# A two-layer transformer kernel: the first layer's attention outputs kept by feature, their division by the softmax sums moved to the next stage

## What is computed

```
def _attn(x, ctx, wq, wk, wv, wo, bo, heads):
    ...
    q = (x @ wq).reshape(b, n, heads, dh).transpose(0, 2, 1, 3)
    k = (ctx @ wk).reshape(b, j, heads, dh).transpose(0, 2, 1, 3)
    v = (ctx @ wv).reshape(b, j, heads, dh).transpose(0, 2, 1, 3)
    a = jax.nn.softmax(jnp.einsum('bhid,bhjd->bhij', q, k) * scale, axis=-1)
    out = jnp.einsum('bhij,bhjd->bhid', a, v)
    out = out.transpose(0, 2, 1, 3).reshape(b, n, heads * dh)
    return out @ wo + bo
...
x = _attn(h1, h1, q1, k1, v1, o1_w, o1_b, heads) + x
...
x = _attn(h2, context, q2, k2, v2, o2_w, o2_b, heads) + x
...
ff = a * jax.nn.gelu(g, approximate=False) @ ff_w2 + ff_b2
```

## Time and profile before

| | us |
|---|---|
| median of 3 runs (lowest, highest) | 3342.19 (3334.15, 3347.52) |
| the profiled execution, its time | 3342.7 |
| its span in the trace | 3341.0 |
| self-attention, from about 207 to 698 | 491 |
| q stage, 698 to 852 | 154 |
| cross-attention, 852 to 1029 | 177 |
| ff stage, 1029 to 1700 | 671 |
| layer 1, 1700 to 3341 | 1641 |

### The profile page before, as it was taken

How to read it: one execution, slowest core, us unless ns; L and a number is a source line. 1 busy time by engine, 2 the same in 40 slices (tenths; PEclk the granted TensorE clock), 3 DMA queues, 4 the chain that set the end, 5 groups by cost and what they waited for, 6 DMA issues and landing times. The chain is left out here.

```text
span 3341.0 us, 47964 instructions
## 1 busy us (share of the span) xinstructions
PE 2936.9 (88%) x15594; PEld 1775.7 (53%) x15594; DVE 2157.7 (65%) x3834; ACT 1892.4 (57%) x3214; POOL 805.5 (24%) x1149
## 2 busy tenths in 40 slices
PE   6989999978696999998959999879978577899999
PEld 5754444457455888886731111111126342788888
DVE  5668888837453444444649999968868685444443
ACT  4328888844353232233549999989975355333322
POOL 2021221114640000000027888200003471200000
PEclk9969999989798999998975555555559898899999
DMA  8663333336762000001567557266723213010000
GB/s 228 211 166 101 106 107 103 90 80 158 165 176 46 10 10 19 9 0 38 152 173 163 128 137 164 32 90 83 97 56 96 79 45 92 26 36 18 25 17 16
DMA packets 358243, 296.57 MB, mean 89 GB/s; under 512 B 175602, under 2 KB 281914, under 8 KB 358058
## 3 DMA queue, kind: packets, MB, share of 16 engines
q1 hardware_dynamic: 347994, 273.93, 34.0%
q0 software_dynamic: 7280, 18.07, 2.1%
q10 hardware_dynamic: 2784, 2.29, 0.4%
HBM read 177.53 MB, written 114.52 MB: 87 GB/s over the span
## 5 line engine op out<-in xcount | busy, mean ns | idle before, releaser
L1591 PE MATMUL nat<-k_stack,q_stack 48*128 48x512 bf16 x640 | 381.0, 605 | 71.5 <-DMA k_stack<-k1w 31.1
L1391 DVE TENSOR_REDUCE neg_max<-nat 128x1 f32<-128x512 f32 x640 | 400.7, 682 | 61.3 <-PE nat L1250 61.2
L1625 DVE TENSOR_REDUCE m_all<-nat 128x1 f32<-128x512 f32 x640 | 423.3, 691 | 18.1 <-PE nat L1591 17.8
L804 POOL TENSOR_TENSOR rstd<-var_eps,neghalf 128x4 f32<-128x4 f32 x48 | 51.9, 1081 | 1588.0 <-DVE var_eps L1028 1588.0
L1645 ACT ACTIVATE nat<-nat,m_all 128x512 f32<-128x512 f32 x640 | 427.7, 2130 | 3.0 <-DVE m_all L1625 2.9
L1645 ACT ACTIVATION_READ_ACCUMULATOR nat<-nat,m_all 128x1 f32 x640 | 403.6, 1674 | 0.0
L1054 DVE SCALAR_TENSOR_TENSOR ff<-outp,bias,gel 128x512 f32<-128x512 f32 x160 | 120.1, 751 | 417.6 <-PE outp L326 417.6
L1325 ACT ACTIVATE probs<-sT 128x1024 f32<-128x1024 f32 x320 | 328.0, 1027 | 93.1 <-PE sT L1259 85.5
L968 ACT ACTIVATE gel<-outp,bias 128x512 f32<-128x512 f32 x160 | 110.0, 688 | 351.6 <-PE outp L326 351.6
L1839 ACT ACTIVATE exps<-sT 128x1024 f32<-128x1024 f32 x320 | 293.4, 1573 | 10.5 <-PE sT L1788 10.5
L972 ACT CAST ff_hi<-ff 128x512 fp32r<-128x512 f32 x160 | 99.2, 620 | 312.3 <-DVE ff L1054 312.3
(11 more groups left out here) (561 smaller groups left out, 7163.3 us busy)
## 6 DMA issues: line engine op xcount, KB each, us to landing
v<-vpad SPq DMA_DIRECT2D x64, 320.0 KB, 2.8
q_stack<-q_part SPq DMA_DIRECT2D x90, 160.0 KB, 5.8
k_stack<-k1w SPq DMA_DIRECT2D x90, 160.0 KB, 10.5
q_stack<-q_hi SPq DMA_DIRECT2D x160, 64.0 KB, 2.5
v_stack<-v SPq DMA_DIRECT2D x40, 256.0 KB, 3.2
q_stack<-q_hi SPq DMA_DIRECT2D x80, 128.0 KB, 2.8
raw<-v SPq DMA_DIRECT2D x16, 640.0 KB, 14.9
k_stack<-k_hi SPq DMA_DIRECT2D x158, 64.0 KB, 2.2
```

What stands on the lines that cost most here:

```text
L1391: dve.tensor_reduce(neg_max[:, n % 2, qt, 2 * pr + ab:2 * pr + ab + 1], nat[(16 * (n + 2) + t) % 3][:, :], AX.X, ALU.max, negate=True).the ...
L1591: pe.matmul(bank[i % NAT][:, :], q_stack[half, slot, g, pr, qt * P:(qt + 1) * P], k_stack[half, slot, g, pr, :], start=True, stop=True).th ...
L1625: dve.tensor_reduce(k.m_all[:, column(i // TILES, i % TILES)], bank[i % NAT][:, :], AX.X, ALU.max, negate=True).then_inc(s["e_max_ready"], 1)
```

## The change

Both attentions of layer 0 stop after `o_ps`: it is copied to a now double `o_sb` (by ACT in self-attention, by DVE in cross-attention) and stored as it is, 128 rows of 2 KB per quad, the sums and padding among them. The transposes, the second copy, the per-quad reciprocal and the multiply go. Instead, once per sample, a DMA loads the 20 rows of sums as an 80x128 tile (`load_sums`), DVE inverts it (`invert`), and another DMA stores it (`store_shares`); these two DMAs are SP's in self-attention and POOL's in cross-attention. In cross-attention the loads of v move from SP's list to POOL's.

The q stage and the ff stage take the form by feature. For each sample SP issues eight DMAs: four bring the output (`attn_T`), four bring the inverted sums, each head's row sent to 16 partitions (`shares`). DVE multiplies the two in three steps of 128x512 (`scale`) before the high and low halves are taken. The twelve transposes of each sample go.

```diff
+        scale = [("scale", m) for m in range(3)] if recips is not None else []
...
-            ahead = {"oT": 1, "oproj": 1, "stats": 1, "norm": 1, "zT": 1, "tail": -1}
-            between = [[("tail", 0)], oT[0:2], oT[2:], oproj[0:2], oproj[2:], [("stats", 0)], [("norm", 0)],
+            ahead = {"oT": 1, "oproj": 1, "stats": 1, "norm": 1, "zT": 1, "tail": -1, "scale": 1}
+            between = [[("tail", 0), *scale], oT[0:2], oT[2:], oproj[0:2], oproj[2:], [("stats", 0)], [("norm", 0)],
...
+            if scale:
+                ahead["scale"] = 3
             body = [("stats", 0), *oT[0:2], items[0], oT[2], ("norm", 0), items[1], items[2], oproj[0], ("double", 0),
-                    zT[0], zT[1], oproj[1], zT[2], oproj[2], oproj[3]]
+                    zT[0], zT[1], oproj[1], zT[2], *scale[0:2], oproj[2], *scale[2:], oproj[3]]
...
-            n_attn = 3 if by_feature else TT + 1
+            n_attn = 8 if scale else 3 if by_feature else TT + 1
+            if scale:
+                shares = sb("shares", [P, 3, TOK])
...
+                    if scale:
+                        heads = rows(attn_in, b * (QUADS * P), QUADS * P).rearrange("(h c) t -> h c t", c=VCOL)[:, 0:DH, :]
+                        spread = rows(recips, b * HEADS, HEADS).unsqueeze(1).broadcast_to([HEADS, DH, TOK])
+                        for tile, src in ((attn, heads), (shares, spread)):
+                            for c in range(2):
+                                sp.dma_start(tile[:, c, :], src[8 * c:8 * c + 8]).then_inc(s["attn_in_loaded"], 16)
+                            for half in range(2):
+                                sp.dma_start(tile[64 * half:64 * half + 64, 2, :], src[16:HEADS]
+                                             ).then_inc(s["attn_in_loaded"], 16)
+                        return
...
+                        elif scale:
+                            act.wait_ge(s["o_scaled"], at["o_scaled"] + b * 3 + m + 1)
...
-                    if kind == "oT":
+                    if kind == "scale":
+                        if m == 0:
+                            dve.wait_ge(s["attn_in_loaded"],
+                                        at["attn_in_loaded"] + b * (16 * n_attn) + 16 * n_attn)
+                        dve.tensor_tensor(attn[:, m, :], attn[:, m, :], shares[:, m, :], ALU.mult
+                                          ).then_inc(s["o_scaled"], 1)
+                    elif kind == "oT":
...
-        recip = sb("recip", [P, 2, TT, 4])
-        o_sb, o_turned = sb("o_sb", [P, TOK]), sb("o_turned", [P, 2, TOK])
-        o_nat = sb("o_nat", [P, 2, TT, 4, DH])
+        o_sb = sb("o_sb", [P, 2, TOK])
+        sums, shares = sb("sums", [TT * HEADS, P]), sb("shares", [TT * HEADS, P])
...
+                def load_sums(b):
+                    for r in range(2):
+                        wait(sp, f"a_o_stored{r}", 16 * ((QUADS * (b + 1) - r + 1) // 2))
+                    sums_of = rows(out, b * (QUADS * P), QUADS * P).rearrange("(h c) t -> h c t", c=VCOL)[:, DH, :]
+                    sp.dma_start(sums[:, :], sums_of.rearrange("h (x t) -> h x t", t=P)
+                                 ).then_inc(s["a_sums_loaded"], 16)
+
+                def store_shares(b):
+                    wait(sp, "a_recip", b + 1)
+                    sp.dma_start(rows(recips, b * HEADS, HEADS).rearrange("h (x t) -> h x t", t=P), shares[:, :]
+                                 ).then_inc(s["a_recip_stored"], 16)
...
-                    if exists(n - 3):
-                        wait(sp, "a_o_normed", n - 2)
-                        sp.dma_start(rows(out, (n - 3) * TOK, TOK).rearrange("(t p) c -> p t c", p=P),
-                                     o_nat[:, (n - 3) % 2].rearrange("p t h c -> p t (h c)")
-                                     ).then_inc(s[f"a_o_stored{(n - 3) % 2}"], 16)
+                    if exists(n - 2):
+                        wait(sp, "a_o_copied", n - 1)
+                        sp.dma_start(rows(out, (n - 2) * P, P), o_sb[:, n % 2, :]).then_inc(s[f"a_o_stored{n % 2}"], 16)
+                    if exists(n - 3) and (n - 3) % QUADS == QUADS - 1:
+                        load_sums((n - 3) // QUADS)
+                    if exists(n - 4) and (n - 4) % QUADS == QUADS - 1:
+                        store_shares((n - 4) // QUADS)
...
-                        if exists(n - 2) and j == 2:
-                            turn_output(n - 2)
...
+                def invert(b):
+                    wait(dve, "a_sums_loaded", 16 * (b + 1))
+                    wait(dve, "a_recip_stored", 16 * b)
+                    dve.reciprocal(shares[:, :], sums[:, :]).then_inc(s["a_recip"], 1)
...
+                        if t == 8 and exists(n - 4) and (n - 4) % QUADS == QUADS - 1:
+                            invert((n - 4) // QUADS)
...
-                    if exists(n - 2) and n % PER == 1 and b + 1 < BATCH:
-                        wait(sp, "x_pv_done", n - 1)
-                        load_v(b + 1)
...
+                    if exists(n - 2):
+                        wait(sp, "x_o_copied", n - 1)
+                        sp.dma_start(rows(out, (n - 2) * P, P), o_sb[:, n % 2, :]).then_inc(s[f"x_o_stored{n % 2}"], 16)
...
-                def turn_output(n):
-                    wait(pe, "x_o_copied", n + 1)
-                    for qt in range(TT):
-                        mm = pe.transpose(o_ps[n % 2][:, qt * P:(qt + 1) * P], o_sb[:, qt * P:(qt + 1) * P], k.ident[:, :])
-                    mm.then_inc(s["x_o_turned"], 1)
...
-                    if exists(n - 1):
-                        wait(act, "x_pv_done", n)
-                        wait(act, "x_o_turned", n - 1)
-                        act.copy(o_sb[:, :], o_ps[(n - 1) % 2][:, :]).then_inc(s["x_o_copied"], 1)
...
+                def load_v(b):
+                    src = rows(v, b * HEADS * CTX_TOK, HEADS * CTX_TOK).rearrange("(x ab k) c -> ab k x c", ab=2, k=CTX_TOK)
+                    for ab in range(2):
+                        pool.dma_start(v_stack[64 * ab:64 * ab + 64, b % 2, :, :, ab, :].rearrange("k g pr c -> k (g pr) c"),
+                                       src[ab]).then_inc(s["xp_v_loaded"], 16)
...
+                def load_sums(b):
+                    wait(pool, "xp_shares_moved", 32 * b)
+                    for r in range(2):
+                        wait(pool, f"x_o_stored{r}", 16 * ((PER * (b + 1) - r + 1) // 2))
+                    sums_of = rows(out, b * (PER * P), PER * P).rearrange("(h c) t -> h c t", c=VCOL)[:, DH, :]
+                    pool.dma_start(sums[:, :], sums_of.rearrange("h (x t) -> h x t", t=P)
+                                   ).then_inc(s["xp_shares_moved"], 16)
+
+                def store_shares(b):
+                    wait(pool, "x_recip", b + 1)
+                    pool.dma_start(rows(recips, b * HEADS, HEADS).rearrange("h (x t) -> h x t", t=P), shares[:, :]
+                                   ).then_inc(s["xp_shares_moved"], 16)
+
+                load_v(0)
+                load_v(1)
                 wait(pool, "x_parts_set", 1)
                 early.load(pool)
                 for n in range(NQ):
@@ -2121,19 +2120,31 @@
                     loader.turn(pool, n)
                     if n < BATCH * TT:
                         early.add(pool, n)
+                    b = n // PER - 1
+                    if b >= 1 and n % PER == 0 and b + 1 < BATCH:
+                        wait(pool, "x_pv_done", PER * b)
+                        wait(pool, "xp_v_loaded", 16 * N_V * (b + 1))
+                        load_v(b + 1)
+                    if b >= 0 and n % PER == 2:
+                        if b >= 1:
+                            load_sums(b - 1)
+                    if b >= 1 and n % PER == 4:
+                        store_shares(b - 1)
+                for b in (BATCH - 2, BATCH - 1):
+                    load_sums(b)
+                    store_shares(b)
+                wait(pool, "xp_shares_moved", 32 * BATCH)
...
-                    r = n % 2
-                    wait(dve, "x_o_turned", n + 1)
-                    wait(dve, f"x_o_stored{r}", 16 * (n // 2))
-                    o = o_ps[r][:, :].rearrange("p (t h c) -> p t h c", t=TT, h=4)
-                    dve.reciprocal(recip[:, r], o[:, :, :, DH]).then_inc(s["x_recip"], 1)
-                    wait(dve, "x_recip", n + 1)
-                    dve.tensor_tensor(o_nat[:, r], o[:, :, :, 0:DH],
-                                      recip[:, r].unsqueeze(3).broadcast_to([P, TT, 4, DH]), ALU.mult
-                                      ).then_inc(s["x_o_normed"], 1)
+                def copy(n):
+                    wait(dve, "x_pv_done", n + 1)
+                    wait(dve, f"x_o_stored{n % 2}", 16 * (n // 2))
+                    dve.tensor_copy(o_sb[:, n % 2, :], o_ps[n % 2][:, :]).then_inc(s["x_o_copied"], 1)
+
+                def invert(b):
+                    wait(dve, "xp_shares_moved", 32 * b + 16)
+                    dve.reciprocal(shares[:, :], sums[:, :]).then_inc(s["x_recip"], 1)
```

(15 more changed lines are left out.)

101 lines of the change are left out of this document (26 added, 75 removed).

## The result

The changed kernel takes 3398.81 us (median of 4 runs, 3397.48 to 3403.97), the kernel before beside it 3344.86; the ratio is 1.0169 with a 95% interval of 1.0141 to 1.0197. Forecast were 3346 us and a range up to 3376. The profiled execution has a span of 3396.1 us, 55.1 more than before.

The account below looks back on a forecast made before the run. The prediction took PE to bound self-attention and a chain of waits the q stage. Self-attention -31, q stage +48, cross-attention -8 and ff -5 made +4 on 3342.7; forecast 3346 us, range 3299 to 3376.

Parts of the forecast that it names:

- L: q stage: a sample's loads take 11.8 us against 5.6 before, 13.2 where POOL's weight loads share the engines.
- Cycle = 13.2 + 7.9: q stage: loads plus DVE's way from scale to the next oT_lo make 21.1 us a sample, where it was 15.4.
- The first sample: q stage: first var_eps comes at 737.6 instead of 722.59, +15, with sample 0's loads starting near 704.5.
- The floor behind it: q stage: with early loads DVE's own chain sets the cycle, 15.4 + 2.0 for scales less 1.4 for waits = 16.0 us.
- 0.5 us less for 30 steady rounds, -15: Cross-attention: without transposes PE needs 2.90 us and ACT 2.98 of a 3.48 us round, saving 15 us.
- lower bound of 0.1 a round: Cross-attention: least gain per round, if the store chain through SP's queue holds; the upper bound was 0.58.
- four round trips: Cross-attention's end: last two samples' sums fetched, inverted and stored serially, 2.4 us per trip, +4.2 net.
- 38 x 0.85: Self-attention: some 38 steady rounds each lose 0.85 us, 32 us less.
- the lower bound: Self-attention: the unit with the turn falls to its neighbour's length, 0.78 us a round off PE.
- R1: q and ff stages: loads spread over all 16 engines, L 5.3 to 7 us, total 3300 us; chance 0.16.
- R2: q and ff stages: a 2 KB row costs 0.10 us, not 0.081, +22, total 3369 us; chance 0.12.
- R3: Attention rounds shrink less: self-attention held at 11.2 us, cross-attention at 3.2, +18 and +7, total 3371 us; chance 0.12.

Follow-up runs that it names:

- e5_by_head: e1_wide with the head as outer index in the first two pieces of a sample's loads, weights' rows following; 3346.18 us, ratio 1.0014.
- e2_attn_only: Changed kernel with inverted sums loaded for sample 0 only in the q and ff stages, so values are wrong; 3357.39 us (one run).
- e13: e5_by_head with the old cross-attention and ff stage, and the q stage's multiply on POOL, for sample b+2 behind sample b's rstd and weights; 3333.80 us, ratio 0.9977.
- e4: Changed kernel with cross-attention storing only the first 256 tokens of each row from sample 1 on; 3395.98 us (one run).
- e7: Changed kernel with the sums and shares of cross-attention's last two samples moved by SP instead of POOL; 3392.85 us, ratio 1.0153.
- e1_wide: Changed kernel with q and ff stage loads taken feature index outermost, on 16 engines, output weights' rows in the same order; 3353.42 us, ratio 1.0035.
- e11_outputs_twice: e5_by_head with the loads of inverted sums reading the outputs a second time instead, so scaling is wrong; 3360.00 us (one run).

## Why the prediction was wrong

**The narrow loads: mechanism right, the size of one term too small.** The term L, 11.8 us for a sample's loads and 13.2 beside POOL's weight loads, measured 15.0 in the round shown (763.04 to 778.04) and 15.8 on average. The price of a row was right, 0.083 us against 0.081. What was mis-sized is what stands around the 128 rows: I allowed 1.4 us, and 1.2 for weights (11.8 and 1.2 make 13.0, where the sum went on with 13.2). The engines' 128 rows at 0.083 are 10.6 us; the other 4.4 are in part the start, since the queues carry only POOL's weight loads from 763 to 765, and in part the stores, issued from 769.3 on, on the same engines (how the 4.4 divide isn't shown). Of "Cycle = 13.2 + 7.9" the 7.9 measured 8.1, from the multiply at 754.91 to the next issue at 763.04. Six cycles of 23.8 on average instead of 21.1 are the +17.

**The first sample came out right by luck.** +15 was forecast to the first `var_eps` and +15.6 measured, but the loads of sample 0 started 32.0 us after the last `nat` of self-attention (675.05 - 643.1), 3.9 earlier than forecast (704.5 - 668.6), since the last store came 24.5 us after that `nat` (667.62) where the forecast had 28.4; and the first two samples' loads took 14.8 and 14.1 us instead of 11.8 each.

**The floor behind it was wrong too, though it cost nothing there.** "Were the loads early, the cycle would be ... 16.0" credited 1.4 us for waits that go with the transposes. e5_by_head shows 18.0 us with almost no wait, e2_attn_only 17.8: DVE's busy time grew by 2.4 us, the multiplies' 2.0 among them, and its short waits, apart from that for the loads, stayed near 3 us: there was no credit. DVE is the bound of this stage as soon as the loads aren't, which e13 confirmed by taking the multiplies away.

**Cross-attention: "0.5 us less for 30 steady rounds, -15" failed.** This step took PE's own work for the path of the round. The rounds did run at 2.9 us where nothing else came between, as forecast, but from first to last `sT` they took 148.9 us, as before. PE no longer bound them all the time: it waited 12.9 us more, mostly for the DMAs of the turned maxima, and ran its matmuls at a lower clock (+11.8 us). My lower bound of 0.1 a round named SP's store chain; the wait was on the six-row DMAs, and e4 shows that half of it goes when the stores are halved. The clock, which I weighed only for the q stage, took the rest. That the clock fell because of the idle stretches is read from the order of the rounds and not tested by itself.

**The end of cross-attention**: four round trips were priced alike at 2.4 us; behind POOL's last store stood its DRAIN of 3.9 us, a step that the sum had at nothing, and from the issue to the next stage's first load it took 6.1. e7, with the DRAIN under the rounds, gives 4.7 us back in the trace.

**Self-attention**: the term "38 x 0.85" measured 35 x 0.68. 0.68 us a round is under the 0.78 that I took for the lower bound: without the turn its unit takes 1.34 us and not its neighbour's 1.24 (why isn't shown), and four rounds at the start gained nothing. The inverts took 0.94 us each, not 0.2 to 0.4, and made the round that held one 0.27 longer.

**The rivals.** R1 fell (197 and 99 GB/s). R2 named landings of 15 us, which came, though not by its price of a row, which held; the stores that it named did share the engines. R3 had self-attention at 11.2 us a round (it is 10.90) and cross-attention 7 us short of the forecast; cross-attention went further than that, and not for its reason. Self-attention's 0.68, the loads' 15.8 and cross-attention's rounds each lie outside the bounds that the forecast gave them, all on the slow side; the range reached only as far as one rival at a time.

## What to carry to other kernels

In this kernel a transfer with an outermost dimension of 8 or 4 kept eight or four engines busy: count rows per engine, not bytes, and look whether the next transfer waits for this one's reader. Reordering the features so that 16 stands outermost, and permuting the weight's rows to match, gave back four fifths of the loss (1.7% to 0.35%). Before pricing work off the busiest engine, find the second chain in the round: in cross-attention the DMAs of the turned maxima stood right behind PE's 0.58 us, and some idle stretches of PE were followed by rounds at half clock.

## What was not expected of the hardware

- Sixteen engines that load 2 KB rows from DRAM together made 224 to 262 GB/s in the second part of a sample's loads (e1_wide, e11_outputs_twice), 14 to 16 each, after 322 to 342 GB/s in the first (e11_outputs_twice, e5_by_head); four or eight made 24.7 each, and with stores in the mix sixteen made 375 GB/s. The reason is open.
- At the end of cross-attention POOL's DRAIN took 3.9 us and held up the next stage, SP's 0.1 us; with SP as the last to finish (e7_late_sums_sp) the next stage began 1.9 us after the last store's issue instead of 6.1.
- Adding 27.6 us of matmul work to PE left the time as it was (3399.03, one run, against 3398.81): what it filled had been idle time and half-speed stretches.
- While POOL multiplied, DVE's `var_eps` of 128x4 took 0.81 to 0.85 us in e13, against 0.17 in the changed kernel. In both rounds shown it ended 0.02 us after the multiply (753.73 and 753.71, 770.21 and 770.19), while DVE's operations beside it kept their length (`bn` 1.67 us in both kernels).
